# Second of three passes of a fused graph network: 32x96 pair scores, 64x64 context products, doubled high and low parts, transposes moved

## The reference

```python
m_left = jnp.einsum('bsh,oh->bso', h, W_left[l])
m_right = jnp.einsum('bsh,oh->bso', h, W_right[l])
u_left = jnp.einsum('bih,bjh->bij', h, m_left) / temper
u_right = jnp.einsum('bih,bjh->bij', h, m_right) / temper
u = u_left * adj_tri + u_left * diag_mask + u_right * jnp.swapaxes(adj_tri, 1, 2)
delta_exp_u = jnp.exp(u) * adj
attention = delta_exp_u / (jnp.sum(delta_exp_u, axis=2, keepdims=True) + 1e-10)
h_lin = jnp.einsum('bsh,oh->bso', h, W_lin[l]) + b_lin[l]
ctx = jnp.matmul(attention, h_lin)
h = jax.nn.relu(_layer_norm(ctx, ln_a[l], ln_b[l]))
```

## Time and profile before

| what | value |
|---|---|
| median of 3 runs | 2915.94 us (2915.21 to 2917.95) |
| the profiled execution's own time | 2916.61 us |
| its span | 2914.6 us |
| PE busy | 2759.4 us, 95% of the span |
| DVE / POOL / ACT busy | 73% / 47% / 39% |
| stage 2, first projection to its last store | about 847 to 1712 us |
| one slot of stage 2 | 26.3 to 26.5 us |

### The profile page before, as it was taken

How to read it: one execution, slowest core, us unless ns; L and a number is a source line. 1 busy time by engine, 2 the same in 40 slices (tenths; PEclk the granted TensorE clock), 3 DMA queues, 4 the chain that set the end, 5 groups by cost and what they waited for, 6 DMA issues and landing times. The chain is left out here.

```text
span 2914.6 us, 59573 instructions
## 1 busy us (share of the span) xinstructions
PE 2759.4 (95%) x23360; PEld 2363.3 (81%) x23360; DVE 2121.5 (73%) x4962; ACT 1138.3 (39%) x2241; POOL 1379.1 (47%) x1255
## 2 busy tenths in 40 slices
PE   8999999999959999999999959999999999999997
PEld 7888999888848888888888847888888888788776
DVE  5788888888847676676677657778777876667765
ACT  2344444434422322232223214444444444554554
POOL 6755765576537555565555534222222223333333
PEclk9999999999979999999999979999999999999998
DMA  5011211121041111011011021111111111111111
GB/s 149 29 51 51 65 61 50 53 65 58 30 125 32 37 52 29 24 52 30 27 48 36 18 72 54 35 38 48 48 48 32 41 48 48 59 54 56 48 60 46
DMA packets 135015, 146.06 MB, mean 50 GB/s; under 512 B 57296, under 2 KB 132688, under 8 KB 134736
## 3 DMA queue, kind: packets, MB, share of 16 engines
q1 hardware_dynamic: 134736, 142.25, 15.9%
HBM read 91.89 MB, written 50.33 MB: 49 GB/s over the span
## 5 line engine op out<-in xcount | busy, mean ns | idle before, releaser
L1135 DVE TENSOR_TENSOR l_val<-l_ring,l_vec 64x384 f32<-64x384 f32 x512 | 284.5, 556 | 76.0 <-PE l_ring L950 69.0
L950 PE MATMUL l_ring<-whi,l_hhi 128*128 128x384 f32 x1152 | 272.7, 345 | 5.8 <-POOL wlo L79 5.8
L1858 POOL TENSOR_TENSOR h_proba<-h_proba,h_mx 128x512 f32<-128x512 f32 x96 | 100.6, 1048 | 349.3 <-DVE h_mx L1717 349.3
L950 PE MATMUL l_ring<-whi,l_hlo 128*128 128x384 f32 x1152 | 263.8, 337 | 0.0
L950 PE MATMUL l_ring<-wlo,l_hhi 128*128 128x384 f32 x1152 | 263.7, 337 | 0.0
L1466 PE MATMUL h_ring<-h_hhi,whi 128*128 128x512 f32 x576 | 241.8, 420 | 17.6 <-ACT h_q L1614 15.2
L1858 POOL TENSOR_TENSOR h_probb<-h_probb,h_mx 128x512 f32<-128x512 f32 x96 | 100.2, 1043 | 324.0 <-DVE h_mx L1717 324.0
L680 POOL TENSOR_TENSOR l_hlo<-l_hf,l_hhi 128x512 fp32r<-128x512 f32 x96 | 128.5, 1364 | 255.5 <-DVE l_hhi L477 255.5
L445 ACT ACTIVATE l_mt<-l_ring 128x512 f32<-128x512 f32 x192 | 114.8, 598 | 292.6 <-PE l_ring L345 292.6
L1466 PE MATMUL h_ring<-h_hlo,whi 128*128 128x512 f32 x576 | 228.4, 396 | 0.0
L1466 PE MATMUL h_ring<-h_hhi,wlo 128*128 128x512 f32 x576 | 228.2, 396 | 0.0
(11 more groups left out here) (213 smaller groups left out, 6720.6 us busy)
## 6 DMA issues: line engine op xcount, KB each, us to landing
l_hf<-xt SPq DMA_DIRECT2D x16, 864.0 KB, 5.2
l_x<-x SPq DMA_DIRECT2D x16, 768.0 KB, 4.5
h_xa<-x SPq DMA_DIRECT2D x32, 384.0 KB, 4.5
h_xb<-x SPq DMA_DIRECT2D x32, 384.0 KB, 5.1
x<-l_zfa SPq DMA_DIRECT2D x8, 768.0 KB, 3.5
x<-l_zfb SPq DMA_DIRECT2D x8, 768.0 KB, 4.3
l_xa<-x SPq DMA_DIRECT2D x16, 384.0 KB, 3.1
l_xb<-x SPq DMA_DIRECT2D x16, 384.0 KB, 3.3
```

Of the source, the lines that this page charges most:

```text
L950: mm = nc.tensor.matmul(ring[k % RING][:, 0:D], hh[:, c, first:first + P], ww[:, c, :], start=(j == 0), stop=(j == len(terms) - 1))
L1135: ins = nc.vector.tensor_tensor(val[half, (g + b) % GRAPHS, 0:D], ring[k % RING][half, 0:D], bias[half, :], ALU.add)
L1858: nc.gpsimd.tensor_tensor(row, row, mx[:, c, ts, :].rearrange("p t h -> p (t h)").unsqueeze(2) .broadcast_to([P, 2 * HP, S]), ALU.subtract ...
```

## The change

- Pair scores: before, 2 sides x 4 tiles x 3 chunks x 2 graphs, 48 products with 64 stationary columns (from `mt`) and 64 moving columns (from `hf`). Now 4 tiles x 3 chunks x 2 graphs x 2 halves, 48 products with 32 stationary columns (from `hf`) and 96 moving columns (from `sides`), which leave out the quarter of each pair block that no mask keeps. `W_left` and `W_right` are passed untransposed for it.
- Context: before, `dt_` was block diagonal over 128x128 and one product did a tile. Now each graph is a 64x64 product, and four of them, two tiles by two graphs, fill the two halves of two banks. Four banks are used, ring[3] is the fourth. The result rows lie in another order after each layer, so the adjacency and the masks are loaded and made for each slot.
- `hhi` and `hlo` have two buffers, one for even and one for odd slots.
- PE's transposes for the next slot stand right behind the pair scores, ahead of the last two values. DVE's casts stand ahead of the third `values_out`, and the deltas between the third and the fourth.

```diff
+            def pair_scores(n):
+                pe.wait_ge(cleared, 1)
+                pe.wait_ge(ml_evac, 2 * KC * (n + 1))
+                pe.wait_ge(d_done, n)
+                for t in range(T):
+                    for c in range(KC):
+                        for b in range(2):
+                            for half in range(2):
+                                g, first = 2 * t + b, S * b + Q * half
+                                mm = nc.tensor.matmul(
+                                    scores[first:first + Q, t * P + Q * half:t * P + Q * half + 3 * Q],
+                                    hf[:, c, g * S + Q * half:g * S + Q * half + Q],
+                                    sides[:, c, g, :, :, :].rearrange("p h w i -> p (h w i)")[:, Q * half:Q * half + 3 * Q],
+                                    start=(c == 0), stop=(c == KC - 1))
+                mm.then_inc(u_done, 1)
...
+                for p in range(2):
+                    for y in range(2):
+                        for b in range(2):
+                            t, out = (2 * y + p, 2 * p + b) if n % 4 < 2 else (2 * p + y, 2 * b + p)
+                            rows = slice(S * b, S * b + S)
+                            mm = nc.tensor.matmul(context_banks[out][S * y:S * y + S, 0:DV], dt_[rows, t, :],
+                                                  val[rows, t, :], start=True, stop=True)
+                    mm.then_inc(c_done, 1)
...
+                projections(n, w0)
+                values(n, SLOT[w0 + 2], range(0, 2))
+                pair_scores(n)
+                if not last:
+                    transposes(n + 1, (n + 1) % 2, s in (0, 3), i + (s == 3))
+                values(n, SLOT[w0 + 2], range(2, 4))
+                context(n)
...
+                    dve.wait_ge(f_done, KC * n + c + 1)
+                    dve.wait_ge(v_done, max(NPROJ * (n - 1), 0))
+                    nc.vector.tensor_copy(hhi[n % 2][:, c, :], hf[:, c, :]).then_inc(hi_done, 1)
...
+                one_side(n)
+                if n + 1 < 4 * iters:
+                    high_parts(n + 1)
+                values_out(n, l, [2])
+                deltas(n)
+                values_out(n, l, [3])
+                normalise(n)
+                apply(n)
...
+                masks(n)
                 if s == 3:
                     final_power(2 * i)
```

More of the change, by code:

```diff
@@ L254, in _, with transposes @@
         def _(pe):
-            def transposes(n, a, src_x, i, freed=None, first=0):
+            def transposes(n, a, src_x, i):
                 if src_x:
@@ L263, in transposes @@
                 for c in range(KC):
-                    if freed is not None:
-                        pe.wait_ge(freed, first + c + 1)
                     for t in range(T):
@@ L268, in transposes, with products @@
                     mm.then_inc(t_done, 1)
-            def values(n, w0, count, bank, free):
-                for k in count:
-                    w = SLOT[w0 + k // T]
-                    first = k % T * P + (S if k >= 2 * T else 0)
-                    free(k)
-                    terms = [(hh, ww, c) for hh, ww in ((hhi, sh.whi[w]), (hhi, sh.wlo[w]), (hlo, sh.whi[w]))
-                             for c in range(KC)]
+            def products(n, w):
+                hi, lo = hhi[n % 2], hlo[n % 2]
+                return [(hh, ww, c) for hh, ww in ((hi, sh.whi[w]), (hi, sh.wlo[w]), (lo, sh.whi[w])) for c in range(KC)]
@@ L278, in values @@
+            def values(n, w, ks):
+                for k in ks:
+                    pe.wait_ge(c_evac, T * n)
+                    if k >= 2:
+                        pe.wait_ge(v_evac, NROW * n + k - 1)
+                    terms = products(n, w)
                     for j, (hh, ww, c) in enumerate(terms):
-                        if soft and k == 0 and hh is hlo:
-                            pe.wait_ge(lo_done, KC * n + c + 1)
-                        mm = nc.tensor.matmul(bank(k)[:, 0:D], hh[:, c, first:first + P], ww[:, c, :],
+                        mm = nc.tensor.matmul(cbank[k % 2][:, 0:D], hh[:, c, k * P:(k + 1) * P], ww[:, c, :],
@@ L366, in slot_masked @@
-                mm.then_inc(u_done, 1)
-                values(n, w0 + 2, range(2, 4), lambda k: cbank[k % 2], free)
-                if not (last and s == 3):
-                    transposes(n + 1, 1 - a, s in (0, 3), i + (s == 3))
-                context(n)
+                for t in range(T):
[8 more added lines that the diff above has]
+                                    start=(c == 0), stop=(c == KC - 1))
@@ L668, in _ @@
-            in_turns(dve, iters, body)
-            for step in FINAL:
-                step(4 * iters - 1, groups - 1, 1)
+            high_parts(0)
+            dve.wait_ge(vec_in[0], 16 * nvec)
+            for n in range(4 * iters):
+                i, s, l = n // 4, n % 4, n % 4 // 2
+                if s == 2:
+                    dve.wait_ge(vec_in[1], 16 * nvec)
+                split_weights(sh, dve, "hi", *weights_of_slot(i, s))
+                done = [(n - 1, 2 * i, 0)] if s == 3 else [(n - 1, 2 * i - 1, 1)] if s == 0 and i else []
+                for m, g, a in done:
+                    final_sum(m, g, a)
+                    final_stats(g)
+                values_out(n, l, range(0, 2))
+                for m, g, a in done:
+                    final_apply(g, a)
+                one_side(n)
+                if n + 1 < 4 * iters:
+                    high_parts(n + 1)
[4 more added lines that the diff above has]
+                apply(n)
```

563 lines of the change are left out of this document (163 added, 400 removed).

## The result

The changed kernel takes 2960.65 us (median of 4 runs, 2959.57 to 2962.56), the kernel before 2916.94 on the same chip (2915.21 to 2918.47): a ratio of 1.0151, interval 1.0138 to 1.0165. It is slower, as predicted. The size is off: +44 us where the forecast was +27.4.

A forecast was written before the change was run, and what follows sets the result against it. PE alone was taken to set the pace (95% busy), with readiness of the context's operands deciding afterwards. Terms -2 + 32 - 1.6 - 1 = +27.4 on 2916.6 gave 2944 us, 0.9% slower; range 2914 to 2972.

The forecast's parts named there:

- The question put: Stage 2, ahead of the context: whether its operands are ready when PE comes to it, not what PE saves.
- The context goes four abreast: Context products on PE: four sets of 64x64 tiles take 1.4 us instead of 2.9, saving 1.5 a slot.
- The scores go four abreast: Pair scores on PE: 24 sets of 32-wide tiles take 2.3 us instead of 2.95, saving 0.65.
- A change of tile shape: PE between scores, context and other products: each switch drains the array, about 0.1 us.
- The chain of 6.6 us: ACT, DVE and POOL from the scores' sides to the context: 6.6 us, casts and deltas held by POOL.
- the other side: Rival: POOL holds DVE neither at third cast nor deltas; chain 5.2 us, kernel 2905 us; chance 0.15.
- Closing slots: Slots where DVE waits for the previous slot's rows: sides S + 22.1, context S + 28.7; +2.3 us, 14 slots, +32.
- Last slot: Slot without casts or POOL beside it: about 24.8 instead of 26.4 us, -1.6; statistics after it, -1.
- The signs of being wrong: Prediction wrong if closing slots aren't longer than plain ones, or PE stays over 95% busy in stage 2.
- Masks and adjacency loads: Two masks on POOL and four adjacency loads, now in every slot: no cost.
- Transposes that wait for `x`: Closing slots: PE's transposes wait 1.5 us for the `x` load but end before the exponential; costs nothing.
- Plain slot: Slots where DVE waits for scores: next context at S + 26.3, PE idles 2.1 us; -0.1 in 16 slots, -2 us.

The follow-up runs named there:

- the fastest kernel: The milder order with the four scalings of `final_apply` moved from DVE to ACT, behind `context_out`: 2871.39 us, ratio 0.9848 to the kernel before.
- the milder order: Changed kernel with transposes between third and fourth value, third value and deltas ahead of casts, `final_apply` last, POOL waiting for all casts: 2886.32 us.

## Why the prediction was right in direction and too small

**Settled by the trace and the runs.** The question put was the right one: not what PE saves, but whether the context's operands are ready.

- *The context goes four abreast.* From its first start to the last it is 1.05 us, before 2.58. The scores start 17.2 to 17.4 us behind it, before 18.55 to 18.7: 1.3 us saved, 1.5 forecast. The Trainium skill ("TensorEngine Tiling (Array Packing)", Tiling Modes) lists 64x64 as four tiles that work in parallel, and the trace agrees: the records start in fours, within 20 ns.
- *The scores go four abreast.* 1.94 us from first start to last for 24 sets, 0.084 a set; 2.3 forecast, from a row of another shape. PE's next product starts 2.12 us behind their first, before 2.95: 0.8 us saved, 0.65 forecast. On PE alone that makes 2.2 us a slot where 2.15 was forecast. It is hidden in closing slots behind DVE. A change of tile shape takes at most 0.1 us, as it stands in the sum: behind the last set of the scores the next product starts after 0.18 us (a set takes 0.08), behind the last set of the context after 0.41 (a set takes 0.33)., which I had read for it, could not show it, since its products all have one shape.
- *The chain of 6.6 us.* 6.46 to 6.49 measured in all slots but three and the last. The parts held by POOL were there about as priced: deltas 1.02 us (0.85 forecast), casts 2.34 (2.25). The rival of a DVE that isn't held ("the other side") fell, and the run with POOL behind the deltas shows that it would have been real: at a chain of 4.9 us the kernel is faster than before.
- *Closing slots.* Sides at S + 21.67 in the slot of 28.12 us (1202.28 - 1180.61), S + 22.1 forecast; context at S + 28.1, forecast 28.7. Mean of the 14 with disturbed ones: 28.64. The term is (28.64 - 26.38) x 14 = +31.6 us, forecast +32. That is an agreement by accident: +24.5 is the undisturbed slot, and the other 7 us are clock, with one late load of `x` among them.
- *Last slot.* 25.22 us instead of 26.44: -1.2, forecast -1.6. Behind the last context 1.8 us fell away, forecast 1; but the first context comes 2.2 us later than before, and the forecast had nothing for it.
- *The signs of being wrong.* Neither came: closing slots are 2 us longer than plain ones, and PE is busy for 90% of the stage, not over 95.
- *Masks and adjacency loads.* No wait of size stands against them in the stage, as said; no run leaves them out.
- *Transposes that wait for `x`.* They do, from 0.2 to 3.0 us in 11 closing slots. "Costs nothing" held where the wait was short, since the sides are late anyway, but not in the slot with 3.0 us: it is idle time too, the clock fell behind it, and the chain took 7.8 us.

**The step that failed** is "Plain slot": "Change: -0.1 a slot, 16 slots, -2 us". Its chain was right. At the full clock a plain slot takes 25.95 to 26.12 us; 26.3 was forecast. The mis-sized term is the price of idle time. I let PE idle 2.1 us a plain slot (measured 1.95 in 14 of 16) and 3 to 5 in closing ones (2.7 to 4.1, the waits for `x` included), and gave it no price but the wait itself, as if the 1.00 of the earlier trace rows would stay. In the trace the clock is at half for 3.41 us about such waits, beginning from 0.7 us ahead of the context to 1.4 behind its start in all cases but one, and whatever PE does there takes twice its time. In this piece of the changed kernel's timeline it is the projections:

```profile
1321.44 1.15 PE L285 MATMUL l_ctx<-l_val,l_dt 64*64 64x385 f32 x9 [2.74 <-DVE l_val L353]
...
1322.99 1.65 PE L257 MATMUL l_ring<-l_hhib,whi 128*128 128x512 f32 x3
...
1324.44 1.48 PE L257 MATMUL l_ring<-l_hhib,wlo 128*128 128x512 f32 x3
```

The same group at the full clock, some us behind another context:

```profile
1448.33 0.84 PE L257 MATMUL l_ring<-l_hhib,wlo 128*128 128x512 f32 x3
```

1.48 us against 0.84; from the start of three such records to that of the next three it is 1.45 us against 0.68. A plain slot with a fall takes 27.5 to 27.7 us, 1.5 more. (A delay there isn't absorbed, since what follows is on PE's own path to the next scores.) The mean of all plain slots is 27.23, and the term +0.85 x 16 = +13.7 instead of -2.

Not all of that is clock. In the first two plain slots the chain takes 7.9 and 7.7 us, because POOL still works on the low parts of later weights (`wlo`, line 68): beside that, the second step of the sides takes 1.84 us in the first of them, where it takes 0.42 elsewhere, and the three casts take 3.60 in the second, where they take 2.34:

```profile
892.65 5.25 POOL L68 TENSOR_TENSOR wlo<-stage,whi 128x1152 fp32r<-128x1152 f32 x2
...
896.34 1.84 DVE L363 TENSOR_TENSOR l_ut<-l_ut 128x256 f32<-128x256 f32 x1
...
922.57 5.55 POOL L68 TENSOR_TENSOR wlo<-stage,whi 128x1152 fp32r<-128x1152 f32 x2
...
926.56 3.60 DVE L347 CAST l_hhib<-l_hf 128x512 fp32r<-128x512 f32 x3 [0.97 <-ACT l_hf L311]
```

The run with ten more products has the same two long chains (8.1 and 8.0 us) at the full clock. They are worth 2.6 us. Before, the second step of the sides was held there too (2.34 us), and PE waited 0.2 us ahead of that context: its own work covered the rest.

The sum, by measured terms: 13.7 + 31.6 - 1.2 = +44.1, and first to last context 861.95 us against 818.1 before, +43.8. Without the falls of the clock and the two long chains it would be 16 x (26.03 - 26.38) + 14 x (28.13 - 26.38) - 1.2 = -5.6 + 24.5 - 1.2 = +17.7. Of the remaining 26 us 2.6 are the long chains, and some 24 the clock, one late load of `x` included. The run with ten more products a slot got 20.5 to 22.3 of them back, with three falls left. So without the clock the forecast of +27.4 would have been 7 us too high (the chain was 0.13 shorter, the scores 0.35, the sides 0.4 earlier): two errors that partly cancel.

What stays open: why some waits are followed by a fall and others of the same length are not. Slots with equal waits of 1.95 us exist with and without it, and no run here tells them apart.

## What to carry to other kernels

When a product gets cheaper, ask first which work covered the chain beside it. Here four operations abreast saved some 2.2 us of PE a slot (context 1.3, scores 0.8), worth 33 us alone; reordering threw this and 44 us more away. Price PE's idle time with what comes behind it: in a plain slot of this kernel a wait of 2 us cost, where the clock fell, 1.5 us more. Where DVE prepares operands for PE, keep POOL off in that stretch by a wait on POOL's side (64 us here), and put scaling that can be anywhere on the engine that idles (15 us here).

## What the runs showed that I had not expected

- *The clock.* Waits of 2 to 2.8 us ahead of the context, once in each slot of 26 to 28 us, bring 22 stretches of 3.41 us at half of the clock in 862 us. With waits of 4.1 us each slot has 6.8 us at half. With waits of 0.7 to 1.3 us there is none behind them: the mean over the stage is 1.00 with DVE's order undone and 1.00 in the fastest kernel, and the two falls of the former stand behind waits of 2.4 us for `x`.
- *Tiles don't wait for the queue.* With neighbours in the queue on the same tile, the first four records still start within 40 ns (within 20 ns where neighbours differ), and the whole takes 1.06 us against 1.05.
- *POOL and casts.* That the third cast is held was in the forecast, from the trace before. What the runs add is the proof: a cast with one input takes 0.43 us alone (three 1.40 us with the pace of the chunks) and up to 1.37 beside POOL's difference, and in the milder order, where POOL waits for all three, none of the 96 is longer. The changed kernel first, then the milder order:

```profile
L347 DVE CAST l_hhia<-l_hf x48: 415/427/1372, 846.2 to 1681.8; 128x512 fp32r<-128x512 f32 x48
...
L348 DVE CAST l_hhia<-l_hf x48: 414/427/430, 844.7 to 1614.5; 128x512 fp32r<-128x512 f32 x48
L348 DVE CAST l_hhib<-l_hf x48: 414/427/430, 869.9 to 1639.5; 128x512 fp32r<-128x512 f32 x48
```

- *Loads of `x`.* Their median from issue to landing was 3.1 us before and is 3.2 in the changed kernel, but single ones take longer: before none over 3.5 us, in the changed kernel two with 4.2 and 4.9, with ten more products four with 4.0 to 5.2. The longest waits of the transposes are those.
